# The front of a one-core attention and mixture-of-experts layer, with its roots, loads, zeros and V's bias in other places

## What is computed

```python
xn = _layernorm(x)                       # eps 1e-5
q, k, v = xn @ Wq.T + bq, xn @ Wk.T + bk, xn @ Wv.T + bv   # 16 heads of 16; rope on q and k
scores = q k.T / 4                       # keys: the first 205 and the last 512 positions only
attn = softmax(scores) @ v
a = attn @ Wo.T + bo
logits = xn @ router_w.T                 # 8 experts; top two, softmax of the two, first one used
f = down(silu(xn @ gate.T) * (xn @ up.T)) * weight
out = x + a + f
```

## Time and profile before

| | |
|---|---|
| median of three runs | 379.91 us |
| the profiled execution, its own time | 379.14 us |
| its span | 377.2 us |
| TensorE busy | 360.5 us, 96% of the span |
| VectorE busy | 332.3 us, 88% |
| ScalarE busy | 265.2 us, 70% |
| GpSimd busy | 66.4 us, 18% |
| TensorE's share of the chain that ended last | 91% |

### The profile page before, as it was taken

How to read it: one execution, slowest core, us unless ns; L and a number is a source line. 1 busy time by engine, 2 the same in 40 slices (tenths; PEclk the granted TensorE clock), 3 DMA queues, 4 the chain that set the end, 5 groups by cost and what they waited for, 6 DMA issues and landing times.

```text
span 377.2 us, 12250 instructions
## 1 busy us (share of the span) xinstructions
PE 360.5 (96%) x4670; PEld 206.2 (55%) x4670; DVE 332.3 (88%) x686; ACT 265.2 (70%) x538; POOL 66.4 (18%) x83
## 2 busy tenths in 40 slices
PE   0899999999999999999999999999999999999995
PEld 0665566776664554655546555455465554543374
DVE  5779789998767999999999999999999999998565
ACT  1533667664446888888888888888888888899910
POOL 5002744333000021020220202122122020110000
PEclk9999999999999999999999999999999999999999
DMA  7999645756411212222132221322313222111116
GB/s 241 401 387 258 149 144 170 235 173 180 132 51 44 61 33 60 62 74 62 45 77 74 60 68 40 90 77 57 88 32 95 58 56 74 34 42 36 32 28 224
DMA packets 30762, 40.58 MB, mean 108 GB/s; under 512 B 10740, under 2 KB 25844, under 8 KB 30128
## 3 DMA queue, kind: packets, MB, share of 16 engines
q1 hardware_dynamic: 28648, 34.62, 30.6%
q0 software_dynamic: 1872, 5.11, 5.6%
q10 hardware_dynamic: 192, 0.13, 0.1%
HBM read 25.78 MB, written 11.70 MB: 99 GB/s over the span
## 4 chain that ended last, share of the span: by engine, by line
PE 91%; DVE 2%; ACT 2%; DMA 2%; issue 1%; SPq 1%; ACTq 0%; DVEq 0%
PE ps L772 22%; PE ps L801 22%; PE ps L699 14%; PE ps L650 7%; PE ps L712 6%; PE ps L577 5%; PE ps L663 5%; DMA bqk<-bqk_in 2%; PE ps L688 2%; PE ps L780 2%; PE ps L566 1%; PE ps L636 1%; PE ps L675 1%; DVE x_sb L1268 1%; PE ps L559 1%
## 5 line engine op out<-in xcount | busy, mean ns | idle before, releaser
L1100 DVE TENSOR_REDUCE mx<-ps 128x1 f32<-128x512 f32 x232 | 150.4, 684 | 4.3 <-PE ps L699 1.8
L1414 ACT ACTIVATE probs<-ps 128x512 f32<-128x512 f32 x192 | 101.8, 599 | 18.4 <-PE ps L801 17.4
L801 PE MATMUL ps<-q_op,k_op 98*32 98x512 bf16 (+1 forms) x1104 | 112.1, 381 | 0.1
L699 PE MATMUL ps<-k_op,q_op 96*32 96x512 bf16 x672 | 76.0, 381 | 0.0
L1103 DVE TENSOR_REDUCE mx_tail<-ps 128x2 f32<-128x410 f32 x116 | 66.9, 577 | 3.2 <-PE ps L712 3.0
L801 PEld LDWEIGHTS ps<-q_op,k_op 98*32 98x32 bf16 (+1 forms) x1104 | 40.0, 96 | 33.2 <-issue 6.6
L772 PE MATMUL ps<-probs,v_op 128*32 128x512 f32 x384 | 52.4, 592 | 0.0
L1414 ACT ACTIVATE dn<-ps 77x512 f32<-77x512 f32 x64 | 34.2, 591 | 8.3 <-PE ps L801 8.2
L491 POOL COPY v_op<-v_all 128x192 f32<-128x192 f32 x16 | 7.0, 444 | 187.7 <-PE ps L772 187.7
L699 PEld LDWEIGHTS ps<-k_op,q_op 96*32 96x32 bf16 x672 | 25.5, 96 | 21.2 <-DVE mx L1100 8.0
L1414 ACT ACTIVATE gu<-ps 128x512 f32<-128x512 f32 x64 | 33.2, 605 | 5.0 <-PE ps L801 5.0
(11 more groups left out here) (141 smaller groups left out, 488.4 us busy)
## 6 DMA issues: line engine op xcount, KB each, us to landing
q_parts<-parts SPq DMA_DIRECT2D x12, 256.0 KB, 3.1
sorted_results<-ys SPq DMA_DIRECT2D x23, 128.0 KB, 2.3
gu<-gu_in SPq DMA_DIRECT2D x1, 2816.0 KB, 13.3
q_op<-q_parts SPq DMA_DIRECT2D x11, 192.0 KB, 3.4
tab<-tab_in SPq DMA_DIRECT2D x1, 2048.0 KB, 11.8
sorted_rows<-xn SPq DMA_DIRECT2D x4, 512.0 KB, 6.3
out<-x_sb SPq DMA_DIRECT2D x8, 256.0 KB, 2.4
xnT<-o_st SPq DMA_DIRECT2D x62, 32.0 KB, 2.3
```

Of the source, the lines that this page charges most:

```text
L699: ins = pe.matmul(bank(t % 2)[r:r + CW, :], q_op[slot][0:KR, P * t + r:P * t + r + CW], k_op[slot][0:KR, 0:NWIDE], start=True, stop=True)
L801: ins = pe.matmul(bank(4 + u % RING)[r:r + w, :], k_op[h % OPS][:, c0 + r:c0 + r + w], q_op[h % OPS][:, QB * b:QB * b + QB], start=True, s ...
L1100: dve.tensor_reduce(mx[:, slot, t:t + 1], bank(t % 2)[:, 0:NWIDE], AX.X, ALU.max).then_inc(wide_reduced, 1)
L1414: act.activation(prob[c][0:rows, QB * b:QB * b + QB], bank(4 + u % RING)[0:rows, :], ACT.Exp, scale=SCALE).then_inc(exp_done, 1)
```

## The change

- **Roots.** Epsilon goes into the root as ScalarE's bias operand, and the `tensor_scalar` goes. VectorE's list is now moments 0, normalize 0, moments 1, normalize 1 and so on, ScalarE's root 0, normalize 0, two copies, root 1 and so on. In the last group too each engine writes two tiles; VectorE copies pair 6 and ScalarE pair 7.
- **Loads.** The identity is a DMA of its own, issued by ScalarE first of all. The rest of the constants and the router's weights come behind `x`. K's and Q's weights are apart, the table is loaded in three parts (`TAB_OF` says which block needs which), the last two behind `gu` and behind the second gather. The down weights are issued by ScalarE, behind its last copy of a pair.
- **Zeros.** `keep_running(n)` is n bf16 matmuls of a zeroed stretch of `q_op[1]` into bank 6, 512 columns each: 16 ahead of the first pair, then 6, 2, 2 and 2 between later steps.
- **Order on TensorE.** All four blocks of the logits in one go, two chunks of V ahead of them, and half of `project(2)` ahead of the slot sums.
- **V's bias.** ScalarE copies V to `v_all` without it (`copy_v`). Two matmuls of `bv` with `wo` just ahead of the first head give `Wo bv` in bank 3, VectorE adds it to the output's bias, and `add_bias` on GpSimd waits for that.
- **Ones.** GpSimd writes `v_all` first, and the three `k_op` once the logits are there.

```diff
@@ SyncE
-                if g == 1:
-                    sp.dma_start(const[:], const_d).then_inc(const_in, 16)
-                    sp.dma_start(rt[:], rt_d).then_inc(rt_in, 16)
-            sp.dma_start(wqk[:, 0:2, :].rearrange("p w n -> p (w n)"), wqk_d).then_inc(wqk_in, 16)
-            sp.dma_start(bqk[:], bqk_d).then_inc(wqk_in, 16)
+            sp.dma_start(wqk[:, 0, :], wqk_d[:, 0:HC * HID]).then_inc(wk_in, 16)
+            sp.dma_start(bqk[:], bqk_d).then_inc(bqk_in, 16)
+            sp.dma_start(rt[:], rt_d).then_inc(rt_in, 16)
             sp.dma_start(wv[:], wv_d).then_inc(wv_in, 16)
-            sp.dma_start(bvo[:], bvo_d.broadcast_to([P, 2 * HID])).then_inc(wv_in, 16)
-            sp.dma_start(tab[:].rearrange("p a n -> p (a n)"), tab_d).then_inc(tab_in, 16)
+            sp.dma_start(const[:, C_TRI:C_END], const_d[:, C_TRI:C_END]).then_inc(const_in, 16)
+            sp.dma_start(bias, bvo_d[:, HID:2 * HID].broadcast_to([P, HID])).then_inc(bvo_in, 16)
+            sp.dma_start(bv_col, bvo_d[:, 0:HID].rearrange("a (m p) -> (a p) m", p=P), allow_slow_non_contiguous=True).then_inc(bvo_in, 16)
...
+            load_tab(0)
+            sp.dma_start(wqk[:, 1, :], wqk_d[:, HC * HID:2 * HC * HID]).then_inc(wq_in, 16)
...
             sp.dma_start(gu[:], gu_d).then_inc(gate_up_in, 16)
+            load_tab(1)
             store_part(0, 0)
-            sp.dma_start(dn[0:80, :], dn_d[0:80, :]).then_inc(down_in, 16)
-            sp.dma_start(dn[80:IH, :], dn_d[80:IH, :]).then_inc(down_in, 16)
             sp.wait_ge(xs_in[1], 16)
+            load_tab(2)
@@ GpSimd
-            for n in range(RING):
-                pool.memset(k_op[n][KR:KM, :], 1.0).then_inc(ones_ready, 1)
+            pool.memset(v_all[:], 1.0).then_inc(ones_ready, 1)
...
+            pool.wait_ge(logits_T_ready, 1)
+            for n in range(RING):
+                pool.memset(k_op[n][KR:KM, :], 1.0).then_inc(ones_ready, 1)
@@ TensorE
+            def keep_running(times):
...
+                for _ in range(times):
+                    pe.matmul(bank(6), q_op[1][:, 0:P], q_op[1][:, 0:QB], start=True, stop=True)
...
+            pe.wait_ge(warm_ready, 1)
+            keep_running(16)
+            pe.wait_ge(ident_in, 16)
+            for pair in (0, 1):
                 turn_pair(pair)
...
+            keep_running(6)
+            for pair in (2, 3):
+                turn_pair(pair)
+            keep_running(2)
+            pe.wait_ge(wk_in, 16)
+            pe.wait_ge(xnT_ready, 1)
+            project(0)
+            keep_running(2)
+            for pair in (4, 5):
+                turn_pair(pair)
+            pe.wait_ge(wv_in, 16)
+            for c in V_ORDER[0:2]:
+                project_v(c)
+            for pair in (6, 7):
+                turn_pair(pair)
+            keep_running(2)
...
             for m in range(HC):
-                for b in range(1, NQB):
+                for b in range(NQB):
                     ins = logits_part(b, m)
...
+            pe.wait_ge(wo_in, 16)
+            pe.wait_ge(bvo_in, 32)
+            for m in range(HC):
+                ins = pe.matmul(bank(3)[:, 0:HID], bv_col[:, m:m + 1].broadcast_to([P, P]),
+                                wo[:, HID * m:HID * m + HID], start=m == 0, stop=m == HC - 1)
+            ins.then_inc(bias_in_psum, 1)
@@ VectorE
-                dve.tensor_scalar(var[:, 4 * g:4 * g + 4], mv[:, 4 * g:4 * g + 4, 1], EPS, None,
-                                  ALU.add).then_inc(var_ready, 1)
+                    dve.bn_aggr(mv[:, t, :], stats[:, t, :]).then_inc(var_ready, 1)
...
+            dve.memset(q_op[1][:, 0:QB], 0.0).then_inc(warm_ready, 1)
...
+            dve.wait_ge(bias_in_psum, 1)
+            dve.wait_ge(bvo_in, 32)
+            dve.tensor_tensor(bias, bank(3)[:, 0:HID], bias, ALU.add).then_inc(bias_ready, 1)
@@ ScalarE
+                act.activation(std[:, 4 * g:4 * g + 4], mv[:, 4 * g:4 * g + 4, 1], ACT.Sqrt, bias=eps[:, 0:1],
+                               scale=1.0).then_inc(std_ready, 1)
...
+            act.dma_start(const[:, 0:C_TRI], const_d[:, 0:C_TRI]).then_inc(ident_in, 16)
...
+            act.dma_start(dn[0:80, :], dn_d[0:80, :]).then_inc(down_in, 16)
+            act.dma_start(dn[80:IH, :], dn_d[80:IH, :]).then_inc(down_in, 16)
```

More of the change, by code:

```diff
@@ L115, in layer @@
         bvo = sb("bvo", [P, 2 * HID])
+        bias = bvo[:, HID:2 * HID]
+        bv_col = bvo[:, 0:HC]
         const = sb("const", [P, C_END])
@@ L522, in add_bias @@
             def add_bias(t):
-                pool.tensor_tensor(x_sb[:, t, :], x_sb[:, t, :], bvo[:, HID:2 * HID], ALU.add
+                if t == 0:
+                    pool.wait_ge(bias_ready, 1)
+                pool.tensor_tensor(x_sb[:, t, :], x_sb[:, t, :], bias, ALU.add
                                    ).then_inc(residual_ready, 1)
@@ L872, in settle, with statistics @@
                 dve.wait_ge(dve_step, steps[0])
-            def moments(g):
-                for t in range(4 * g, 4 * g + 4):
+            def statistics(first, last):
+                for t in range(first, last):
                     if t == 0:
@@ L1078, in _ @@
             experts()
-            dve.wait_ge(ones_ready, RING + 1)
-            dve.wait_ge(wv_in, 32)
-            for n in range(NCH):
-                add_bv(n)
             rest(0)
```

148 lines of the change are left out of this document (82 added, 66 removed).

## The result

The changed kernel takes **384.51 us** (median of 4 runs, 384.12 to 386.07); the kernel before, run beside it, 379.98 us (379.86 to 381.81). The ratio is 1.0123, with an interval from 1.0092 to 1.0154: 4.5 us slower, where 2.6 us faster was forecast.

What follows compares the result with a forecast made beforehand. TensorE, busy 96% of the span and 91% of the ending chain, was taken as the bound. Front -3.75, gather wait +0.3, bias +0.87 gave -2.6 us: 379.91 to 377.3 us, range 375.9 to 379.2.

Steps and rivals of the forecast that it cites:

- The loads are no bound: In the front: `x`, the identity and K's weights, 2.4 MB, land by 9.8 us; K's weights are used at about 11.7.
- would lose some where they run beside `gu`: Down weights on ScalarE's queue: they gain no bandwidth there and lose some beside the gate and up weights; no size given.
- The gather's term: At the first gathered rows: TensorE waits 0.3 us, bounds 0 and 0.8, with the gather taking 4.9 us.
- should be emptier: At the first gather: DMA engines less loaded, since a megabyte of the table moves behind the second gather; wait 0.3 us.
- The clock's rival: Front: TensorE's pauses drop the clock to 1.2 GHz, costing 2.5 us, so 379.8 us, no change; chance 0.08.
- The slower rival: ScalarE's queue: DMA issues there hold ScalarE, delaying the logits' copy, routing and gathers; up to 388 us; chance 0.04.
- the front: Start up to the logits: first pair at 7.4 us, logits from 18.45, 2.9 us earlier, turned logits at 21.8.
- 0.87 us for the bias: Between the last expert's `down` and the first head: two matmuls of V's bias add 0.87 us, all on the path.
- the move as a block: The program after the front: everything shifts together with TensorE, VectorE's backlog too; first head 2.6 us earlier.
- TensorE asked for rows 0.9 us earlier than forecast: First gathered rows: the forecast had TensorE ask for them at 37.2 us instead of 40.94, 3.75 us earlier.
- the 9.28 us from the turned logits to the sums: Time to the slot sums before; less 0.87 for V, plus 1.74 for half a projection: 10.15 us, ending at 31.95.

Runs made afterwards that it cites:

- e1: The changed kernel with the down weights issued by SyncE again, behind the first store of K's parts: 378.22 us, ratio 0.9961.
- e4: The kernel before with its down weights issued by ScalarE behind its last copy of a pair: 379.87 us, ratio 1.0013.
- e2: The changed kernel with part 1 of the table issued ahead of the gate and up weights: 378.9 us, ratio 0.9971.
- e3: The changed kernel with the down weights still on ScalarE, but issued only once the gate and up weights have landed: 387.42 us, ratio 1.0201.
- e7: e5 with the gate and up weights in short rows too and part 1 of the table ahead of them: 380.05 us, ratio 1.0013.
- e10: e5 without the two bias matmuls and VectorE's addition, V's bias left out of the output: 376.14 us, ratio 0.9925.
- e11: e5 with half of `project(2)` behind the slot sums again, as before the change: 378.97 us, ratio 0.9973.
- e5: e1 with the down weights loaded in rows of 2 KB, even and odd experts apart: 377.31 us, ratio 0.9941.
- e15: e1 with the gate and up weights in two halves of columns, 128 partitions each, on SyncE's and ScalarE's queues: 378.63 us, ratio 0.9966.
- e13: e1 with the gate and up weights in two halves of 64 partitions, on SyncE's and ScalarE's queues: 385.75 us, ratio 1.0153.
- e16: e1 with the gate and up weights in two halves of 64 partitions, one behind the other on SyncE's queue: 385.08 us, ratio 1.0139.
- e14: The changed kernel with all on SyncE's queue, the down weights between two 64-partition halves of the gate and up weights: 388.33 us, ratio 1.0246.
- e9: e5 without the 28 matmuls of zeros and the memset that feeds them: 378.66 us, ratio 0.9968.

## Why the prediction was wrong

- **"The loads are no bound"** is the step that failed. It was worked out for the loads up to K's weights only. For the down weights the prediction priced the issue on ScalarE (1.2 us assumed, 1.29 measured) and not the transfer, which was moved from behind the gate and up weights to beside them. The earlier trace rows even held a hint: 387 and then 258 GB/s, and the lower figure falls where the down weights run (from 31 to 34 us the kernel before moved 232 GB/s on DMA engines that were busy throughout). The prediction's own sentence that the down weights "would lose some where they run beside `gu`" was left without a price, and it leaves out what the gate and up weights would lose. Measured: 23.3 us instead of 13.3 for the gate and up weights; e1 takes it away by moving the down weights back (11.6 us), and e4 brings it about in the kernel before (21.9).
- **The gather's term** was 0.3 us between 0 and 0.8, on the ground that the DMA engines "should be emptier". The wait was 4.98 us. The first gather takes 3.2 to 12.8 us in these runs, by what is in flight; the 4.9 of the earlier trace rows was one point of that, and no bound.
- **A wait was missing.** The change put part 1 of the table behind the gate and up weights, and VectorE's rotation, ScalarE and the turned rows hang on it: 1.45 us directly (e2 removes it, and 5.6 us of the time go with it).
- **The clock's rival** was looked for in the pauses of the front. In the profiled execution of the change it cost 2.8 us behind the stall instead; in the front it did fall in the profiled executions of e3 and e7.
- **The slower rival** had the right queue, chance 0.04, and the wrong mechanism: the issues never held ScalarE.
- **What held:** the front (logits and turned logits within 0.1 us; the first pair too, but for another reason), 0.87 us for the bias (0.86, e10), the move as a block behind the expert stage's start. TensorE asked for rows 0.9 us earlier than forecast, because the 9.28 us from the turned logits to the sums contained about 0.85 us of waiting for lanes (sums of 1.53 us before, 0.68 after), which half a projection now fills; e11 shows it from the other side.
- With the down weights on SyncE in short rows (e5) the time is 377.31 us, the forecast 377.3. That the sum and that kernel meet is partly luck: in its profiled execution, which took 376.23 us, the wait for rows is 0.98 us instead of 0.3, against the 0.9 us just named.

## What to carry to other kernels

A load that is moved to another queue is moved in time: write down what is in flight beside it, how many partitions each of the two covers, and who waits for the transfers behind both. Loads to 64 or 80 partitions are best kept away from wide ones and from small gathers, and a wide load that has to be cut is cut by columns, not by partitions (e15 against e13). A low rate in a slice whose DMA engines are busy is a sign of such a load, and can be seen in the profile before anything is moved. Work that waits for nothing belongs ahead of the first use of gathered rows, since their arrival varies by more than one step of TensorE.

## What was not expected of the hardware

- 64 partitions on one queue: 214 and 216 GB/s, later 197 (e16, e14); 80 partitions on one queue: 208 and 218 (e1, e5); 128 partitions: 411 (kernel before); 128 partitions on two queues at once: 381 (e15); 128 and 80 partitions beside each other: 242 (the change); two halves of 64 on two queues at once: 276 and 229 (e13), which no account given here explains.
- A gather of 128 rows of 1 KB: 3.2 us beside little (e3's first), 5.1 to 5.6 beside the down weights in rows of 2 KB (e5, e10), 6.7 beside them in rows of 16 KB at its start (e1), 9.1 with the change, 11.5 beside the down weights and the table throughout (e3), 12.6 to 12.8 beside loads cut to 64 partitions (e13, e14, e16).
- The granted clock in the profile's windows reads 1.00 from 5 to 15 us in e9, where the transposes take 1.94 and 1.97 us, twice the 1.06 that they take after zeros. At a program's start the level has to be read from like instructions.
